# A state-space and routed-FFN block: the last batch in two time halves, with FFN steps placed later

## What is computed

```python
x = x + tanh(g_xattn) * ssm(ctx, layernorm(x), ...)
x = x + tanh(g_ffn) * ffn(layernorm(x), Wr, U, V, attr, Wa)

# ssm: channels e = 0..511, states n = 0..15, time t = 0..511
u     = silu(conv4(in_proj @ ctx) + conv_b)
dt_lo, B, C = split(x_proj @ u)            # 16, 16 and 16 rows
delta = softplus(dt_proj @ dt_lo + dt_b)
state[e,n,t] = state[e,n,t-1] * exp(delta[e,t] * A[e,n]) + delta[e,t] * u[e,t] * B[n,t]
y[e,t] = sum_n C[n,t] * state[e,n,t] + D[e] * u[e,t]
result = (y * silu(z)).T                   # z = layernorm(x)

# ffn: 32 slots of rank 16, the best two are used
sc = h @ Wr.T ; g = softmax(sc) on the top 2, renormalised
out = sum_s g[s] * (h @ U[s]) @ V[s]
return out * (0.9 + 0.2 * (g @ sigmoid(attr @ Wa)))
```

## Time and profile before

| what | us |
|---|---|
| median of three runs | 624.99 (624.39 to 625.16) |
| the profiled execution's own time | 624.96 |
| its span | 623.2 |
| last scan ends (550.52 + 1.21) | 551.7 |
| from there to the end of the span | 71.5 |
| GpSimd's `du` of phases 9 to 15, start | 313.17, 343.82, 375.35, 411.46, 446.00, 476.63, 508.15 |

### The profile page before, as it was taken

How to read it: one execution, slowest core, us unless ns; L and a number is a source line. 1 busy time by engine, 2 the same in 40 slices (tenths; PEclk the granted TensorE clock), 3 DMA queues, 4 the chain that set the end, 5 groups by cost and what they waited for, 6 DMA issues and landing times.

```text
span 623.2 us, 9369 instructions
## 1 busy us (share of the span) xinstructions
PE 538.7 (86%) x3410; PEld 415.3 (67%) x3410; DVE 467.7 (75%) x775; ACT 362.0 (58%) x574; POOL 437.2 (70%) x253
## 2 busy tenths in 40 slices
PE   6643979798868899999989999999988989986987
PEld 2142869777767687768777777677776868674443
DVE  3517989878848999788889999778779797944330
ACT  3343786857735667575756767566666676432311
POOL 0056999979996878669988788589978787741000
PEclk9765999999987899999999999999999999998899
DMA  3196000115220001035120000153000000000001
GB/s 83 54 359 232 2 0 2 35 51 192 101 69 1 1 1 52 1 116 210 35 85 2 18 1 19 62 197 102 17 2 18 1 19 1 17 18 1 18 17 50
DMA packets 17408, 35.19 MB, mean 56 GB/s; under 512 B 5441, under 2 KB 5953, under 8 KB 17362
## 3 DMA queue, kind: packets, MB, share of 16 engines
q1 hardware_dynamic: 17362, 34.60, 16.1%
HBM read 30.13 MB, written 4.46 MB: 56 GB/s over the span
## 4 chain that ended last, share of the span: by engine, by line
PE 38%; POOL 24%; DVE 15%; issue 10%; ACT 8%; DMA 3%; SPq 1%; DVEq 0%; POOLq 0%; ACTq 0%
POOL state L437 14%; PE p_s L575 10%; DVE state L1029 9%; PE p_y L593 7%; POOL dbu L428 6%; PE p_f L622 3%; ACT da L799 3%; PE p_tr L548 3%; PE p_v L631 3%; PE p_pr L521 3%; DMA xs<-in_x 2%; PE p_s L631 2%; POOL du L417 2%; POOL diag_b L407 1%; PE p_s L514 1%
## 5 line engine op out<-in xcount | busy, mean ns | idle before, releaser
L437 POOL TENSOR_TENSOR state<-state,c_bc 128x1024 f32<-128x1024 f32 x128 | 302.1, 2366 | 87.7 <-DVE state L1029 87.5
L1029 DVE TENSOR_TENSOR_SCAN state<-da,p_s 128x512 f32<-128x512 f32 x192 | 230.4, 1210 | 24.7 <-PE p_s L575 23.4
L575 PEld LDWEIGHTS p_s<-diag_b,du_t 128*128 128x128 f32 x1536 | 196.6, 198 | 26.7 <-issue 22.1
L575 PE MATMUL p_s<-diag_b,du_t 128*128 128x128 f32 x1536 | 209.8, 282 | 0.7 <-ACT du_t L775 0.7
L799 ACT ACTIVATE da<-delta,a_neg 128x512 f32<-128x512 f32 x192 | 136.2, 716 | 104.9 <-DVE state L1029 104.8
L593 PE MATMUL p_y<-ident,state 128*128 128x128 f32 x1024 | 144.2, 274 | 0.0
L593 PEld LDWEIGHTS p_y<-ident,state 128*128 128x128 f32 x1024 | 119.1, 142 | 10.1 <-issue 8.6
L1029 DVE TENSOR_TENSOR_SCAN state<-p_s,dbu 128x512 f32<-128x512 f32 x64 | 77.1, 1210 | 2.1 <-POOL dbu L428 2.1
L428 POOL TENSOR_TENSOR dbu<-du,b_bc 128x1024 f32<-128x1024 f32 x32 | 75.6, 2361 | 0.1
L799 ACT ACTIVATE p_s<-delta,a_neg 128x512 f32<-128x512 f32 x64 | 43.7, 688 | 28.9 <-DVE state L1029 28.7
L622 PE MATMUL p_f<-u_sb,h_t 128*128 128x512 f32 x96 | 47.7, 603 | 5.0 <-DVE gw L1118 5.0
(11 more groups left out here) (189 smaller groups left out, 621.6 us busy)
## 6 DMA issues: line engine op xcount, KB each, us to landing
c_bc<-bc_rows SPq DMA_DIRECT2D x32, 512.0 KB, 5.0
b_bc<-bc_rows SPq DMA_DIRECT2D x8, 512.0 KB, 4.5
xs<-in_x SPq DMA_DIRECT2D x16, 256.0 KB, 8.3
out<-ot SPq DMA_DIRECT2D x12, 256.0 KB, 2.0
cx<-in_ctx_t SPq DMA_DIRECT2D x4, 512.0 KB, 3.6
u_sb<-in_u_w SPq DMA_DIRECT2D x1, 1024.0 KB, 11.5
v_sb<-in_v_w SPq DMA_DIRECT2D x1, 1024.0 KB, 13.4
out<-state SPq DMA_DIRECT2D x4, 256.0 KB, 2.0
```

Of the source, the lines that this page charges most:

```text
L437: eng.tensor_tensor(pair, pair, c_bc[:, 2 * p:2 * p + 2, :], ALU.mult).then_inc(po_cs, 1)
L575: mm = eng.matmul(p_s[g % BANKS][:, t * P:(t + 1) * P], du_t[:, f % 2, t, :], diag_b[:, i, t, :], start=(t == 0), stop=(t == Q - 1))
L1029: eng.tensor_tensor_scan(slot(g), decayed, added, 0.0, ALU.mult, ALU.add).then_inc(ve_scan, 1)
```

## The change

- `PHASE` becomes a list with a time window. The phases 0 to 11 stay. The last batch's four phases of 512 steps become eight of 256: channel blocks 0 to 3 over the first half, then 0 to 3 over the second. Each instruction of these phases keeps its count and works on half the columns; loops over time blocks of 128 have two turns rather than four. Together there are 20 phases (`F = 20`), and 16 tiles (`TILES`).
- The state at the middle has to be carried: for each pair of states of the first half GpSimd copies the last column into `carry` before it multiplies by C, and the scans of the second half start from it.
- After the first half, rows 0 to 255 of the last batch are complete, so tiles 12 and 13 pass through the FFN inside the phase loop (mid phases 17 and 18). Only tiles 14 and 15 are left for the close, which is written anew.
- FFN steps are placed later in every phase: `normed` and `turn_h` from the end of the phase before to states 1 and 2; scores from state 2 to 4; `best_two` from scans 2, 3 to 4, 5; `gates` from scans 4, 5, 6 to 6, 7, 8, where the third part now stands behind `combine` and the fourth to sixth around `gate_y`; the first two blocks of `h @ U` from state 8 to 10, and the third from 10 to 11, behind `skip`. `turn_gated` goes the other way, from state 2 of the next phase to state 15.
- GpSimd makes the bias of the FFN's layernorm behind the power; VectorE no longer does, and waits for neither.
- At the start, `x` of batch 0 is loaded ahead of the C rows of pairs 5 to 7, the statistics of z move from behind scans 0 to 3 to behind scans 8 to 11, and GpSimd's scale of z of batch 0 from behind pair 5's product with B to ahead of pair 6.

The diff, cut to its core:

```diff
+    PHASE = [(b, k, 0, L) for b in range(B - 1) for k in range(Q)]
+    PHASE += [(B - 1, k, c0, H) for c0 in (0, H) for k in range(Q)]
+    F = len(PHASE)
+    SPLIT = Q * (B - 1)
+    EARLY = TILES - 2
...
-            for p in range(2, PAIRS):
+            for p in range(2, 5):
                 broadcast_c(0, p)
             for k in range(Q):
                 load_x(0, k)
+            for p in range(5, PAIRS):
+                broadcast_c(0, p)
...
             def times_c(f, p):
...
+                pair = state[:, g % RING:g % RING + 2, 0:w]
+                if c0 + w < L:
+                    eng.tensor_copy(carry[:, k, 2 * p:2 * p + 2], pair[:, :, w - 1]).then_inc(po_carry, 1)
+                    eng.wait_ge(po_carry, PAIRS * (f - SPLIT) + p + 1)
+                eng.tensor_tensor(pair, pair, c_bc[:, 2 * p:2 * p + 2, c0:c0 + w], ALU.mult).then_inc(po_cs, 1)
...
                 eng.tensor_tensor(fr[:, i, 0:1], fmv[:, i, 1:2], minus_half[:, 0:1], ALU.pow).then_inc(po_fs, 1)
+                eng.wait_ge(po_fs, 2 * T + 1)
+                eng.tensor_scalar(fr[:, i, 1:2], fmv[:, i, 0:1], fr[:, i, 0:1], -1.0, ALU.mult, ALU.mult).then_inc(po_fs, 1)
...
                         if mid >= 0:
-                            scores(mid)
-                        if tail >= 0:
-                            turn_gated(tail)
-                    if n == 4:
+                            turn_h(mid)
+                    if n == 4:
+                        if mid >= 0:
+                            scores(mid)
...
-                    if n == 8 and mid >= 0:
-                        times_u_weights(mid, [0, 1])
-                    if n == 9 and f + 5 < F:
+                    if n == 9 and f + 5 < BLOCKS:
                         in_projection(f + 5)
                     if n == 10 and mid >= 0:
+                        times_u_weights(mid, [0, 1])
+                    if n == 11 and mid >= 0:
                         times_u_weights(mid, [2])
...
-                    if n == 15 and f >= Q:
-                        turn_h(f - Q)
+                    if n == 15 and mid >= 0:
+                        turn_gated(mid)
...
+                first = 0.0
+                if c0:
+                    eng.wait_ge(po_carry, PAIRS * (f - Q - SPLIT) + n // 2 + 1)
+                    first = carry[:, k, n:n + 1]
+                eng.tensor_tensor_scan(slot(g)[:, 0:w], decayed, added, first, ALU.mult, ALU.add).then_inc(ve_scan, 1)
...
-                    if f == 0 and n < Q:
-                        z_statistics(n)
+                    if f == 0 and 8 <= n < 8 + Q:
+                        z_statistics(n - 8)
```

462 lines of the change are left out of this document (217 added, 245 removed).

## The result

The changed kernel takes 651.18 us (median of four runs, 649.02 to 653.5) against 625.08 us for the kernel before in runs beside it; the ratio is 1.0418, 95% interval 1.0391 to 1.0446. Forecast were 643 in a range of 617 to 656, and slower with 0.72. The profiled execution took 653.5 us with a span of 651.8; that of before, 624.96 with 623.2.

The account below looks back on a forecast made before the run. TensorE was taken to bound the phases, idling 0.6 to 2.3 us in each. Start -6.5, phase 4 -5.5, gates +10, halves +51, close -37, clock +6 gave +18 on 624.96: 643 us, range 617 to 656 (own range 634 to 649).

Parts of the forecast that it names:

- rival (c): TensorE's clock falls in nearly every loop, full phases too: +12 more, 655 us; chance 0.12.
- The close, -37: After the last scan, two tiles left instead of four and a half: 34.4 us against 71.5, range 32 to 38.
- The start, -6.5: At the start, no wait for `x`, so phase 1's projection comes some 10 us earlier; range -8 to -3.
- Rival (d): At the start, `x` still lands at 47 since transfers share the same engines: +6.5, 649 us; chance 0.10.
- The end of phase 4, -5.5: VectorE's 7.30 and TensorE's 3.62 us waits go, through GpSimd's bias and the moved `turn_h`; range -7 to -2.
- The later gates, +10: In full phases `h @ U` waits for a late `gw`: +2 in five phases, +0.5 in phase 8; range -3 to +13.
- The half phases, +51: From phase 11 to the last scan, 194.6 us against 143.65, with half-phase loops of 22.75, or 23.05 with `carry`.
- the clock, +6: TensorE's clock falls behind gaps in half of seven half phases, 1.7 us lost each; between nothing and +20.
- The wait on GpSimd: VectorE's step on `z_sum`, 2.27 us before, sits out GpSimd's current instruction, and this wait moves with it.
- (b): Late gates are harmless as VectorE gets far ahead; full phases cost 0, half phases 21.5: 615 us; chance 0.16.
- (a): Floor of the mechanism: start -8, phase 4 -7, full phases +6, last batch and close +9, no clock: 625; chance 0.16.
- (e): Scans starting from `carry` count as having two SBUF inputs and wait for GpSimd: 30 us, 672; chance 0.03.

Follow-up runs that it names:

- run 1: Kernel before with only the start changed (x loaded earlier, statistics of z behind scans 8 to 11, scale of z later): 622.3 us, ratio 0.9957.
- run 12: Kernel before with start change, GpSimd's bias and first FFN tile late, statistics of z behind scans 4 to 7, scale behind `du` 1: 601.9 us, ratio 0.9627.
- Run 2: Kernel before with only the bias of the FFN's normalisation moved from VectorE to GpSimd: 613.0 us, ratio 0.9816.
- run 11: Kernel before with start change and GpSimd's bias, and the first FFN tile alone at the late places: 603.6 us, ratio 0.9666.
- run 5: Changed kernel with the FFN steps of the phases put back at their old places; halves, start and bias stay: 617.9 us, ratio 0.9884 to the kernel before.
- Run 3: Kernel before with only the middle FFN steps (scores, best two, exponential, gates, `h @ U`) moved later: 646.2 us, ratio 1.0343.
- run 6: Changed kernel with scores and gates in the transposes' bank, except in phases turning B, so `h @ U` needn't wait for `gw`: 646.6 us.
- run 7: Changed kernel with five unread 512-column products ahead of `h @ U` in half phases, filling the gap: 647.2 us, ratio 1.0388 to the kernel before.
- run 8: Changed kernel without the state carried from the first time half to the second: 649.9 us, ratio 1.0376 to the kernel before.

## Why the prediction came out as it did

The sign, the mechanism and the range were right; the time was 8 us short, and 651.2 lies outside the 634 to 649 that the forecast gave itself as its own range, nearer to the 655 of rival (c). In the traces the difference is +28.6 against +18: the last batch was 13 us short, and 4 us too much on the full phases took part of that back by luck. Point by point, by its own terms:

**The close, -37.** Measured -36.8. The steps worked out from the old close's rows were sound: `h @ U` twice took 5.4 and 3.4 us as forecast. As written they add up to 34.2 and not 34.4; measured are 34.65. The old close had 15.7 us of TensorE idle (55.8 busy of 71.5), not some 18.

**The start, -6.5.** Measured -4.4 in the trace and -2.7 alone (run 1), the latter outside the range of -8 to -3. The projection came as early as forecast, 10.6 us. The mis-sized term is GpSimd's scale of z, set at 0.5 (or 2.4 later in its row): ScalarE waited 8.78 us for it, and decays 14 and 15 and the copy of `du` 1 stand behind that wait on the same engine. Run 12 moved the scale and the wait was gone, but it brought `du` 2 forward by only 2.0 of the 3.3 us that were short in run 1; what holds the rest is open. Rival (d) falls with run 12, where `x` is there by 44.71. Its price was wrong too: with the statistics behind scan 8, at 54.5, an `x` that lands at 47 would have cost nothing.

**The end of phase 4, -5.5.** Measured -6.1, right in size and wrong in one of its two causes. The prediction gave the bias and the move of `turn_h` together. Run 2 shows that the bias does nothing there (31.51), run 11 that the move of the first tile does it all (25.28).

**The bias elsewhere, 0.** This step failed. "In the other phases the same wait, 1 to 2.8 us on VectorE, hides behind TensorE" is true of VectorE, but it overlooks who else waits for the bias: `normed`, the turn of `h`, and the turn of `zh` that needs their bank. TensorE's idle of 0.58 us ahead of that turn was in the trace of before, in phase 10, one of ten such waits with 8.6 us in all. Run 2 puts the worth of the bias at 12 us in all, 0.8 of it in a plain phase.

**The later gates, +10.** Measured +5.7 in the six phases, where the error on the bias shows: against run 5, with the bias and the old places, these phases cost 206.2 - 196.7 = +9.5. That this is so near to +10 is partly luck. Against run 5, phases 7, 10 and 11 cost 2.4 to 2.5 us each, phase 9 only 0.5 and phase 6 nothing, where +2 was forecast for each, and phase 8 cost 2.1, where GpSimd's bound was to hold it to 0.5. Run 3, the step by itself, has 33.42 us for the plain phase against 33.6 forecast. The idle ahead of `h @ U`, forecast at 2 to 3 us, is 1.70 with 0.42 ahead of `in_projection`. "The wait for `gate_y` ahead of `skip` is then covered by `h @ U`, and cannot pay it back": right as far as it goes; run 6 showed the other side of it, that it stands directly behind and would take over.

**The half phases, +51, and the clock, +6.** Together 57, measured 70. TensorE's work of a half phase was right (19.2 forecast, 19.3 to 19.5 in run 5), and so was its idle ahead of `h @ U` (3.1 forecast, 2.5 to 3.3). What was short is the clock. The prediction's own steps, from the product of state 8 in phase 11 (403.29 in the changed trace) over each `h @ U` to the last scan, show it:

| step | forecast | measured | four instructions of the `h @ U` it begins with |
|---|---|---|---|
| to phase 11's `h @ U` | 6.2 | 6.0 | - |
| to phase 12's | 28.5 | 30.6 | 3.78 |
| to phase 13's | 23.05 | 23.2 | 1.98 |
| to 14's, 15's, 16's | 23.05, 23.05, 22.75 | 24.9, 26.1, 25.2 | 3.67, 3.78, 3.53 |
| to 17's, 18's | 22.75, 22.75 | 26.1, 24.9 | 3.78, 3.59 |
| to the last scan | 22.5 | 27.0 | 3.78 |

Where the clock kept its level the forecast holds to 0.2 us; where it fell, the step is 1.8 to 3.4 us longer, and the last one 4.5. "I take half of the seven with a loss of 1.7" should have been six of the seven half phases and phase 11, at about 2.2 (run 7). In the last step phase 19's `skip` also waits 1.77 us for `x`. The turning bank took 0.69 to 0.81 and not 0.45 in each. Rival (c), the clock in nearly every loop, was right for the half phases and for phase 11. In the full phases before that the clock fell behind one gap ahead of `h @ U`, 2.25 us in phase 7, where it cost no time: in runs 6 and 8 the four instructions kept their 1.98 us behind the same gap, and the period was the same.

**The wait on GpSimd.** The peculiar step on `z_sum` came along in the full phases, with 1.29 us, but not in the half ones (0.24), since `combine` itself waits 0.63 us for Ln. In the chain of 4.2 us "a pair at 1.28" has a second way beside it, ScalarE's table load (1.28 us, full or half) and Ln, and `combine`; by chance they end within 0.2 us of each other in the half phase shown.

**Rivals.** (b) falls with run 3, whose plain phase costs all that was forecast. (a) was right about the full phases as measured (+6 against +5.7) and fell on the last batch and the close, +9 against +33.4. (d) falls with run 12, (e) with run 8. What did hold is the sentence behind the sum: the halves move the same work from a close into phases that each lose more. Run 5 sharpens it. With no gap ahead of `h @ U` in the half phases and the clock at 1.00 from `du` 14 on, the halves still lose 9 to 10 us, so it isn't only what each phase loses.

## What to carry to other kernels

When a wait is moved or taken away, list every wait that stands on the same engine in the next few steps with the time at which its releaser is done: here `gw` and `x` ended within 2 us of each other, the waits on `hug` and the bank came up more than 10 us later in the same phase, and only putting all the steps back brought the 33 us. A step that "hides" on its own engine isn't free: follow its result through the engines behind it up to the bottleneck, as the bias of 0.2 us was worth 12. And a bundle of edits hides its good parts: taken alone, start and bias gained 2.7%, while the bundle lost 4.2%.

## What the runs showed of the hardware

- An idle of 3.30 us ahead of `h @ U` was followed by instructions at half speed (four in 3.78 us against 1.98), and the granted clock of the half phases from `du` 14 on was 0.87 to 0.93. With the gap filled by useless products it was 1.00, and the phase was shorter in spite of them (24.2 us with 4.3 us of them, against 25.4). Behind gaps of 1.70 and 1.79 us in the full phases the four instructions kept their 1.98 and 0.63 us.
- Between these the length of the gap alone did not decide. Four instructions took 3.63 us behind a gap of 2.25 and 1.98 behind one of 2.53 in the same trace, and 1.98 behind the same 2.25 in runs 6 and 8; behind 2.37 us in the close the clock kept its level in the trace of before and fell in that of run 1, whose close is 2.6 us longer.
- Halving the columns of a scan takes it from 1.21 us to 0.69, not to 0.61, and with a start value in SBUF to 0.74; GpSimd's pair product goes from 2.36 to 1.27, but the bias and the power on one column take it 0.27 and 0.55 us in full and half phases alike. ScalarE's table loads, 1.28 us each, don't shrink, and two of them stand in each phase, full or half.
